# A fused transformer layer: one feed-forward chunk a slot, the upper operand stack in two pieces, work moved off VectorE, V kept on chip

## The reference

```python
# layer 0: attention with 16 heads of 16, then a gated feed-forward of 1024
x = x + a_alpha * attention(gamma * rmsnorm(x) + beta) @ W_o.T
h = gamma2 * rmsnorm(x) + beta2
x = x + f_alpha * (silu(h @ gate_w.T) * (h @ hidden_w.T) @ out_w.T + out_b)
# layer 1: gated feed-forward, quantised activations, ternary weights
h = x * scale * rsqrt(mean(x * x) + eps)
val, gate = split(h @ up_w.T)
h = val * gelu(gate)
y = act_quant(h) @ weight_quant(down_w).T + x
```

## Time and profile before

| what | value |
|---|---|
| runs | 1106.47, 1107.0, 1108.77 us (median 1107.0) |
| profiled execution | 1111.97 us, its span 1109.9 us |
| PE busy | 1039.5 us (94%) |
| DVE, ACT, POOL busy | 771.1 (69%), 562.0 (51%), 346.8 us (31%) |
| chain that ended last | PE 75%, DMA 8%, DVE 6%, issue 4%, SP's queue 4% |
| mean granted TensorE clock | 0.977 |

### The profile page before, as it was taken

The page is one execution under the profiler, slowest core; times in us unless marked ns, Lnnn a source line. Parts: engine busy times, 40 slices in busy tenths (PEclk is TensorE's granted clock), DMA queues, the critical chain, the costliest instruction groups (busy, mean ns, idle before and its releaser), DMA issues.

```text
span 1109.9 us, 19253 instructions
## 1 busy us (share of the span) xinstructions
PE 1039.5 (94%) x6775; PEld 719.9 (65%) x6775; DVE 771.1 (69%) x1557; ACT 562.0 (51%) x1260; POOL 346.8 (31%) x414
## 2 busy tenths in 40 slices
PE   7779889999999999999899999988989999899997
PEld 6324246755775675677467657754878778788775
DVE  5657776678568757966875786677647787466775
ACT  5246656557566655755575566456552333132221
POOL 2401123324242333324133323211332443243331
PEclk9679989999999999999999999999999999999998
DMA  8363524163316315230641533070310111002111
GB/s 261 129 104 112 114 79 135 39 112 101 111 23 127 116 59 106 90 127 12 102 153 59 61 100 131 15 149 20 97 53 29 59 55 32 29 30 63 58 54 38
DMA packets 89375, 92.71 MB, mean 84 GB/s; under 512 B 11856, under 2 KB 86616, under 8 KB 88256
## 3 DMA queue, kind: packets, MB, share of 16 engines
q1 hardware_dynamic: 87248, 89.59, 30.6%
q10 hardware_dynamic: 2032, 1.90, 0.6%
HBM read 61.68 MB, written 29.78 MB: 82 GB/s over the span
## 4 chain that ended last, share of the span: by engine, by line
PE 75%; DMA 8%; DVE 6%; issue 4%; SPq 4%; POOL 1%; ACT 1%; POOLq 0%; DVEq 0%; ACTq 0%
PE gen L1178 30%; PE core L1178 13%; PE pvb L1308 9%; PE core L1267 8%; PE core L1296 7%; DMA kst<-parts_d 6%; SPq L357 4%; PE gen L1520 2%; DVE negmax L936 2%; PE gen L1252 1%; PE pvb L1512 1%; PE pvb L1316 1%; DMA parts_d<-qk 1%; DMA shift_d<-shift 1%; DVE qs L1128 1%
## 5 line engine op out<-in xcount | busy, mean ns | idle before, releaser
L936 DVE TENSOR_REDUCE negmax<-core 128x1 f32<-128x512 f32 x512 | 339.4, 685 | 181.5 <-PE core L1267 180.4
L719 ACT ACTIVATE p<-core 128x512 f32<-128x512 f32 x512 | 278.8, 599 | 147.2 <-PE core L1296 145.9
L1267 PE MATMUL core<-kst,qst 96*128 96x512 bf16 x512 | 201.0, 395 | 36.4 <-DVE negmax L936 18.3
L1178 PE MATMUL gen<-hs,wgh 128*128 128x256 f32 x1536 | 217.6, 292 | 9.6 <-DVE a L993 9.6
L1178 PEld LDWEIGHTS gen<-hs,wgh 128*128 128x128 f32 x1536 | 193.3, 189 | 47.0 <-DVE a L993 14.7
L1178 PE MATMUL core<-wup,hp 128*128 128x512 f32 x768 | 190.6, 397 | 0.9 <-POOL hp L659 0.9
L610 POOL TENSOR_TENSOR a<-a 128x256 fp32r<-128x256 f32 x128 | 94.7, 740 | 289.1 <-ACT a L737 286.6
L1296 PE MATMUL core<-qst,kst 99*128 99x512 bf16 x512 | 157.6, 384 | 2.4 <-DMA qst<-shift_d 1.1
L1178 PEld LDWEIGHTS core<-wup,hp 128*128 128x128 f32 x768 | 140.0, 189 | 29.2 <-issue 0.9
L1267 PEld LDWEIGHTS core<-kst,qst 96*128 96x128 bf16 x512 | 49.5, 97 | 123.4 <-DVE negmax L936 51.7
L1308 PE MATMUL pvb<-p,vst 128*32 128x512 f32 x1024 | 128.0, 619 | 0.0
(11 more groups left out here) (159 smaller groups left out, 1230.6 us busy)
## 6 DMA issues: line engine op xcount, KB each, us to landing
parts_d<-qk SPq DMA_DIRECT2D x30, 384.0 KB, 2.7
v_d<-v SPq DMA_DIRECT2D x8, 1024.0 KB, 4.0
vst<-v_d SPq DMA_DIRECT2D x16, 512.0 KB, 4.8
qst<-parts_d SPq DMA_DIRECT2D x96, 64.0 KB, 2.3
qst<-parts_d SPq DMA_DIRECT2D x48, 128.0 KB, 4.4
kst<-parts_d SPq DMA_DIRECT2D x48, 128.0 KB, 7.5
kst<-parts_d SPq DMA_DIRECT2D x91, 64.0 KB, 2.3
xr<-in_x_dram SPq DMA_DIRECT2D x8, 512.0 KB, 4.1
```

The costliest lines, as they stand in the source:

```text
L719: act.activation(p32[:, ring(b, m), k * S:(k + 1) * S], stb[k], ACT.Exp, scale=SCALE).then_inc(s["exp_"], 1)
L936: dve.tensor_reduce(negmax[:, n // TT, n % TT:n % TT + 1], smb[n % 2], AX_X, ALU.max, negate=True).then_inc(s["smax"], 1)
L1178: last = pe.matmul(out_, l, r, start=start and i == 0, stop=stop and i == len(passes) - 1, **kw)
L1267: pe.matmul(smb[n % 2], qst[0:KROWS, h, q * P:(q + 1) * P], kst[0:KROWS, h, :], start=True, stop=True).then_inc(s["smax_mm"], 1)
```

## The change

- `T_GH` gives every chunk a slot of its own: chunks 0 to 5 stand one slot earlier (z 13 to 18), chunks 6 to 15 where they were. `T_DOWN` follows. The two banks of the chunks are swapped, and the waits that guard them are adapted.
- The upper stack tile comes in two pieces of 4 heads, 12 DMAs each. The first (heads 8 to 11) is issued behind `shift(i, 3)` and ahead of `shift(nxt, 0)`, and needs only 48 of the 64 scores matmuls of the running batch; the second stands where the whole tile stood. In the first iteration both stand there.
- V has two buffers on chip, `v0` for even batches and `v1` for odd ones. `v_d`, its store and both loads are gone. `v_high` writes the buffer that `weighted` reads. GpSimd sets the ones of `v1` once.
- `affine` of the first norm goes from VectorE to ScalarE (for batches 1 to 7). The scaling of the second half of the feed-forward is split into a copy out of PSUM on ScalarE (`y_out`) and a multiplication on GpSimd. The addition of the first half of the first residual goes to GpSimd, which adds two waits to `qk_rest`.
- `shift_turn` and `shift_parts` of batch 0 come ahead of the first maxima of their slot, for all four groups.

```diff
-    T_GH = [T_OT + 13 + n - (n > 5) for n in range(NCH)]
+    T_GH = [T_OT + 12 + n for n in range(NCH)]
...
-        v_d = nc.dram_tensor("v_d", (B, P, TT, H, VW), F32).ap()
...
         def gh_bank(b, n):
-            return gen[0] if b == B - 1 else gen[n % 2]
+            return gen[0] if b == B - 1 else gen[(n + 1) % 2]
...
+        STACK = ("stack_first", "stack0_ld", "stack1_ld", "stack2_ld")
...
-            def stack(b, tile):
+            def stack(b, tile, p0=0, p1=2):
...
-                pieces = ((0, GROUP, "stack_first"), (GROUP, HT, "stack0_ld")) if tile == 0 else ((0, HT, "stack1_ld"),)
+                pieces = ((0, GROUP, STACK[2 * tile]), (GROUP, HT, STACK[2 * tile + 1]))[p0:p1]
                 for h0, h1, name in pieces:
                     need_sp("st_mm", 2 * STEPS, b - 1, 4 * (tile * HT + h1))
...
                 if prev:
-                    need_sp("yt", 2, last, 0)
+                    need_sp("x2_", 2, last, 0)
...
                 if here:
-                    v_load(i, 1)
                     shift(i, 1)
...
                 if here:
                     shift(i, 3)
+                    if prep:
+                        stack(nxt, 1, 0, 1)
                 if prep:
-                    need_sp("v_h", TT // 2, nxt, TT // 2)
-                    sp.dma_start(v_d[bass.ds(nxt, 1), ...
-                    v_load(nxt, 0)
                     shift(nxt, 0)
...
                 if here and prep:
-                    stack(nxt, 1)
+                    stack(nxt, 1, 1, 2)
...
+            def first_residual(b):                       # POOL, z 5
+                need(pool, "xr_load", 16, b, 16)
+                need(pool, "x2_st", 16, b, 0)
+                need(pool, "xt_", 2, b, 1)
+                pool.tensor_tensor(x1[:, 0:2, :], xt[0]..., xr[:, 0:2, :], ALU.add).then_inc(s["x1a"], 1)
...
             def second_residual(b, c):                   # POOL
...
+                if c == 1:
+                    y = h32[:, 1, :].rearrange("p (t d) -> p t d", t=2)
+                    pool.tensor_tensor(y, y, al[:, D:2 * D]..., ALU.mult).then_inc(s["ym"], 1)
+                    need(pool, "ym", 1, b, 1)
...
+            def affine(b):                               # ACT, z 4, batches 1 to 7
+                need(act, "cur_set", 1, b, 1)
+                need(act, "x2_", 2, b - 3, 2)
+                for k in range(KD):
+                    need(act, "xt1", KD, b, k + 1)
+                    act.activation(h32[:, k, :], gen[XT_BANK[k]][:, :], ACT.Identity, bias=..., scale=...)...
+
+            def y_out(b):                                # ACT, z 31
+                need(act, "y_mm", NCH, b, NCH)
+                need(act, "h32_2", KD, b, KD)
+                act.copy(h32[:, 1, :], gen[Y_BANK][:, :]).then_inc(s["yt"], 1)
...
             def qk_rest(b, j):                           # DVE
                 need(dve, "qk_h", 2 * KD, b, j + 1)
+                if j < 2:
+                    need(dve, ("x1a", "x1_")[j], 1, b - 2, 1)
...
-                    for b in at(z, T_DOWN[2 * KF - 1] + 1):
-                        second_scaling(b, 1)
...
             def gate_hidden(b, n):                       # PE
                 if n == 0:
                     need(pe, "hl2", KD, b, KD)
+                    need(pe, "qk_r", 2 * KD, b + 2, 3)
+                if n == 1:
                     need(pe, "v_h", TT // 2, b + 2, 1)
```

More of the change, by code:

```diff
@@ L637, in iteration @@
                         pool.wait_ge(s["kones"], 1)
+                    if i == -1 and z == Z_REST + 2:
+                        pool.wait_ge(s["cw2_t"], 1)
+                        pool.wait_ge(s["wt_t"], 1)
+                        pool.memset(v1[:, :, :, DH:VW], 1.0).then_inc(s["v1_ones"], 1)
+                    for b in at(z, T_OP[0] + 1):
+                        first_residual(b)
                     for b in at(z, T_BIAS):
@@ L795, in iteration @@
                         o_high(b)
+                    for b in at(z, T_DOWN[2 * KF - 1] + 1):
+                        y_out(b)
+                    for b in at(z, T_H1):
+                        if b > 0:
+                            affine(b)
                     if i == -1 and z == Z_XN0:
@@ L1037, in iteration @@
                             heads_out(b, m // (2 * KT))
-                    if i == -1 and z == T_TURN[0]:
-                        shift_parts(0, 0)
+                    for g, t in enumerate(T_TURN):
+                        for b in at(z, t):
+                            if b == 0:
+                                shift_parts(b, g)
                     for b, m in stream(z, T_MAX):
@@ L1258, in scores_max @@
             def scores_max(b, n):
-                for first, name in ((0, "stack_first"), (TT * GROUP, "stack0_ld"), (TT * HT, "stack1_ld")):
+                for first, name in ((TT * GROUP * g, STACK[g]) for g in range(NG)):
                     if n == first:
@@ L1301, in weighted @@
                 g, kt = m // (2 * KT), m % (2 * KT) // 2
-                if kt == 0 and g % 2 == 0:
-                    need(pe, f"v{g // 2}_ld", 16, b, 16)
+                if kt == 0 and g == 0:
+                    need(pe, "v_h", TT // 2, b, TT // 2)
                 if kt == 0:
@@ L1307, in weighted @@
                 for j in range(GROUP):
-                    last = pe.matmul(pvb[j * VW:(j + 1) * VW, :], vst[:, kt, GROUP * g + j, :],
+                    last = pe.matmul(pvb[j * VW:(j + 1) * VW, :], vbuf[b % 2][:, kt, GROUP * g + j, :],
                                      p32[:, ring(b, m - 1 + j // 2), (j % 2) * S:(j % 2 + 1) * S], start=(kt == 0), stop=(kt == KT - 1))
@@ L1421, in iteration @@
                     turned = [(b, g) for g, t in enumerate(T_TURN) for b in at(z, t)]
-                    if (0, 0) in turned:
-                        shift_turn(0, 0)
+                    for b, g in turned:
+                        if b == 0:
+                            shift_turn(b, g)
                     for b, m in stream(z, T_MAX):
```

87 lines of the change are left out of this document (45 added, 42 removed).

## The result

The changed kernel takes 1073.52 us (median of 4 runs, 1072.77 to 1077.58), the kernel before 1107.2 us beside it. The ratio is 0.9701, 95% interval 0.9675 to 0.9728: 33 us faster. The forecast was 1074 us. The profiled execution has a span of 1071.4 us against 1109.9, which is 38.5 us less; that of before had lain 5 us above its median.

A forecast was written before the change was run, and what follows sets the result against it. TensorE was taken as the bound, held mid-program only by maxima, upper stack and gated product. 14.0 + 5.2 + 7.0 + 5.6 + 3.9 - 1.5 - 1.2 = 33.0 us off 1107.0 gave 1074 us, range 1064 to 1090.

The forecast's parts named there:

- Upper stack and the half clock behind it: z 2 waits for the stack go, 14.0 us; the half-speed slots after them in iterations 0 and 1, 5.2 us.
- Rival C: Iteration 0, z 2: the early stack piece lands late because 24 DMAs share busy queues; 1081 us, chance 0.07.
- One chunk a slot, with iteration 8: Product waits at z 20 go, 7.0 us; iteration 8's two product waits and lower clock, 5.6 us.
- the wait left at z 23: Iteration 8: a third wait, for the scaling of the first half, was forecast to stay.
- Second scaling off VectorE: z 31: maxima come 0.65 us earlier in iterations 2 to 7, 3.9 us; GpSimd's new addition costs 1.2 us.
- rival B: GpSimd and VectorE additions block each other before z 9 and at z 31; 1092 us, in part 1082; chance 0.18.
- V on chip: 2 MB a batch of traffic goes, but TensorE waits for no V transfer: 0 us, bounds -1.4 to +5.
- three waits: 160 to 760 us: TensorE held only by reductions of maxima, the upper stack's landing and VectorE's part of the gated product.
- Rival E: z 5: later x2 delays shift(i, 1) in SyncE's queue, 6.1 us in seven iterations; 1117 us, chance 0.03.
- Turns of batch 0: TensorE turns batch 0's maxima first and waits for the last reduction: three slots, 1.5 us cost, bounds 0 and 3.
- rival D: Half clock has other causes, and z 0 and z 20 waits pass to the next limit; 1086 us, chance 0.10.
- 1.0 from iteration 0's z 2 on: Expected sign in the profile after: full granted clock from z 2 of iteration 0 onward.

The follow-up runs named there:

- the moves with the shift ahead: Kernel before with only the work moved from VectorE to ScalarE and GpSimd, and shift(i, 1) issued ahead of x2's store and V's loading: 1104.63 us, ratio 0.9993.

## Why the prediction was right, and where it was not

- *Upper stack and the half clock behind it:* 14.0 + 5.2 = 19.2 us forecast, 17.4 measured alone (15.0 to 19.7 by its interval). The mechanism is as told: the piece landed in time in iteration 0 too, with the full clock behind it. In the change its last transfer landed at 56.3 us and TensorE reached z 2 at 59.6. Rival C is excluded by z 2 of iteration 0.
- *One chunk a slot, with iteration 8:* 7.0 + 5.6 = 12.6 forecast, 11.7 measured (8.0 to 15.5). Both terms show in the trace, and the wait left at z 23, which was to stay, fell from 1.67 to 0.72 us.
- *Second scaling off VectorE:* 3.9 less 1.2 forecast, 0.4 measured in company, within the noise. The 0.6 us an iteration are there; the step that was mis-sized is the cost. It lay not where rival B had it: VectorE's addition takes 1.80 us beside GpSimd's, but the transposes of z 9 wait for `xn` once in the middle, 0.7 us, just as before the change. It lay at z 5 (1.8 us) and at the start of layer 1 (1.1 us).
- *V on chip:* 0 forecast with bounds -1.4 to +5; 0 alone, 3.5 without the moves (the turns included), 17.9 with them. This is the step that failed, and its sentence was "The store was 4.9 us ahead of the shift, so this is covered." Two things ate the lead: with the stall of z 1 and z 2 gone the shift comes sooner after the store (3.8 us with the stack in two pieces), and the moves make x2 1.8 us later, not 1.2, so 2.0 us are left. And what counts is not when the store of x2 was issued but when the last of x2, `al` and V lands (table below). With 3.8 us of lead x2 has already landed, and where V goes through DRAM it is V that lands last. The sign was there: the prediction named three waits "only", but the same view has the one of 0.5 us for `shift_d`.
- *Rival E* (slower, 1117) had the right place and the right chain. Its delay of 3.5 us a time was too high: with V through DRAM it was 1.7 to 3.2 us in six iterations, and the lower clock that it had behind each wait came in one, iteration 7 (730.0 to 733.4 us). Given 0.03, it was one edit away: the change escaped it because V's way left the queue in the same change.
- *Turns of batch 0:* -1.5 forecast; about -2 in iteration 0, nothing measurable in the time.
- *Clock (rival D in part):* "1.0 from iteration 0's z 2 on" was wrong. 3.9 us of the 38.5 in the spans were gained ahead of iteration 0, in iteration -1 (which only prepares batch 0), where no term of mine stands. The slow stretch there ran from 35.1 to 59.0 us before and from 42.7 to 56.3 after. A second one, of 3.4 us at z 6 of iteration 0 (79.5 us), went as well.

So the two large terms were right in kind, and the experiments confirm them; together they gave 28.8 us of the 31.8 forecast. The small ones were each off, one up and one down: -0.4 us instead of -2.7 for the moves, and -3.5 for V and the turns together instead of +1.5. That makes 3.9 us where 1.2 were forecast. That these two errors, 3.0 and 2.7 us, cancel is luck. By the kernels in order, chunks and stack -28.8, V and turns -3.5, moves -0.4, give -32.7 of the measured 33.

## What to carry to other kernels

When a stall is removed, recompute the distance of every pair of transfers around it, since what was issued well ahead may now be in flight together; a small transfer on which the bound engine waits belongs ahead of the large ones in its queue. A part that is worth nothing alone, or loses, says nothing of its worth in company: take it out of the whole as well, and try the order in the queue before rewriting a data path, since here moving a few issues was worth as much as keeping 16.8 MB on chip.

## What the runs showed of the hardware that was not expected

The store of `shift_d` is 16 x 3 x 128 values of bfloat16, 12 KB (the 64 KB in one expectation was wrong). It takes 1.4 us with nothing in flight in most cases, 2.9 to 4.0 us behind a store and a load issued 1.5 to 2 us ahead of it, and 5.3 us behind three. The traces also hold when each transfer landed. Below, these times for `shift(i, 1)`, in us after the issue of its store; a minus is a landing ahead of it:

| kernel, iteration | x2 | `al` | V | the store itself |
|---|---|---|---|---|
| before, 4 | -0.9 | 1.1 | 2.5 | 2.6 |
| before, 5 | -1.1 | 0.9 | 2.5 | 4.0 |
| V on chip alone, 5 | -1.0 | 0.9 | none | 1.4 |
| the change, 4 | 1.2 | 2.8 | none | 3.0 |
| the change, 5 | 2.9 | 3.8 | none | 3.9 |
| the change with V through DRAM, 5 | 1.8 | 3.7 | 5.1 | 5.3 |
| the change with x2 behind the shift, 5 | issued later | 1.9 | none | 2.1 |

The pattern holds widely. Of the 84 such stores (iterations 2 to 7 of all fourteen kernels), 77 landed within 0.2 us of the later of two times: 1.4 us after their own issue, or 0.2 us after the last transfer issued ahead of them had landed. So it is less the number of bytes ahead than the last landing ahead that sets the time. The other seven, among them the second row, took 0.6 to 1.4 us longer. All seven are in iterations 2 and 5. In the change these two are slow for another reason: x2 itself lands 4.9 us after its issue there and 3.2 in the others. Why these two iterations differ stays open. All these transfers were issued by SyncE; whether one issued by another engine would hold the store up in the same way was not tested.

The stretches at half clock are not where the program alone would put them. With the turns left out, the one at 97.3 us was gone and one at 793.6 us had come; a stretch of 3.4 us costs up to 1.7 us. Single runs of the kernel before spread over 13 us, and much of such a spread goes with the clock: of the twelve runs of the moves with the shift ahead, the nine with a mean granted clock of 0.980 or more took 1099.2 to 1110.1 us, the three with 0.969 to 0.974 took 1111.2 to 1112.8. A profile may therefore be several us off its kernel's median by this alone (a span of 1099.0 us for the moves with the shift ahead, median 1104.6), and terms under some 3 us are read from slots, not from the time.
